# One run of kv products and adjacent attention halves in a linear-attention kernel

## What is computed

```python
def feature_map(x, orf):
    proj = x @ orf.T / d_k ** 0.25
    norm = jnp.sum(x * x, axis=-1, keepdims=True) / (2.0 * math.sqrt(d_k))
    return (jnp.exp(proj - norm) + EPS) / math.sqrt(m)
q = feature_map(split(x @ Wq.T + bq), orf)
k = feature_map(split(x @ Wk.T + bk), orf)
v = split(x @ Wv.T + bv)
kv = jnp.einsum('nlm,nld->nmd', k, v)
ksum = jnp.sum(k, axis=1)
buf = jnp.concatenate([kv, ksum[..., None]], axis=-1)
out = jnp.einsum('nlm,nmd->nld', q, buf)
out = out[..., :-1] / out[..., -1:]
...
return out @ Wo.T + bo
```

## Time and profile before

| | us |
|---|---|
| median of 3 runs | 1294.16 |
| lowest, highest | 1293.69, 1294.86 |
| the profiled execution | 1294.25 |
| its span | 1292.4 |
| PE, DVE, ACT, POOL busy | 1271.0, 940.0, 701.2, 327.8 |

### The profile page before, as it was taken

The page is one execution under the profiler, slowest core; times in us unless marked ns, Lnnn a source line. Parts: engine busy times, 40 slices in busy tenths (PEclk is TensorE's granted clock), DMA queues, the critical chain, the costliest instruction groups (busy, mean ns, idle before and its releaser), DMA issues.

```text
span 1292.4 us, 24909 instructions
## 1 busy us (share of the span) xinstructions
PE 1271.0 (98%) x8626; PEld 958.5 (74%) x8626; DVE 940.0 (73%) x1775; ACT 701.2 (54%) x1403; POOL 327.8 (25%) x617
## 2 busy tenths in 40 slices
PE   9999999999999999999999999999999999999986
PEld 8767787777877678776787768876788767887655
DVE  6599765886668875788657886587875788657876
ACT  5557535564356743657336663367534665446534
POOL 0102332024310333103421034211253022420043
PEclk9999999999999999999999999999999999999999
DMA  6658314773146821567215762257612686036611
GB/s 232 147 137 222 95 47 110 180 184 88 58 115 164 201 67 51 135 163 189 62 58 130 181 168 67 64 130 204 158 46 72 144 208 151 27 83 146 162 54 65
DMA packets 82749, 160.33 MB, mean 124 GB/s; under 512 B 17856, under 2 KB 36416, under 8 KB 82112
## 3 DMA queue, kind: packets, MB, share of 16 engines
q1 hardware_dynamic: 68880, 139.78, 43.7%
q10 hardware_dynamic: 9648, 16.85, 3.5%
q0 software_dynamic: 4096, 2.11, 0.7%
HBM read 39.13 MB, written 16.78 MB: 43 GB/s over the span
## 4 chain that ended last, share of the span: by engine, by line
PE 87%; ACT 5%; DVE 4%; issue 3%; POOL 0%; ACTq 0%; POOLq 0%; DVEq 0%
PE ps L946 26%; PE ps L909 18%; PE ps L959 8%; PE ps L1009 8%; PE ps L932 5%; PE ps L934 5%; PE ps L933 5%; PE ps L977 4%; PE ps L964 4%; ACT features L663 2%; PE ps L1035 2%; ACT x_hi L631 1%; PE ps L904 1%; DVE squares_turned L819 0%; ACT unit_hi L644 0%
## 5 line engine op out<-in xcount | busy, mean ns | idle before, releaser
L663 ACT ACTIVATE features<-ps 128x512 f32<-128x512 f32 x512 | 279.0, 604 | 249.3 <-PE ps L959 192.2
L565 POOL DMA_DIRECT2D stacks<-norm_rows x128 | 69.7, 548 | 530.0 <-DVE norm_rows L834 283.9
L959 PEld LDWEIGHTS ps<-orf_stack,stacks 98*128 98x128 f32 x1024 | 131.3, 191 | 29.8 <-issue 21.7
L909 PE MATMUL ps<-Wo_hi,stacks 128*128 128x512 f32 x448 | 150.4, 402 | 0.0
L636 ACT ACTIVATE values_then_attention<-ps 128x512 f32<-128x512 f32 x64 | 38.3, 599 | 198.0 <-PE ps L934 195.0
L775 DVE TENSOR_TENSOR den<-den,features 128x512 f32<-128x512 f32 x186 | 128.1, 689 | 12.8
L959 PE MATMUL ps<-orf_stack,stacks 98*128 98x128 f32 x1024 | 132.0, 272 | 0.0
L1009 PE MATMUL ps<-features,kv_ksum 128*32 128x512 f32 x1024 | 123.1, 598 | 3.4 <-ACT features L663 2.2
L811 DVE SCALAR_TENSOR_TENSOR unit_lo<-ps,cols,unit_hi 128x512 fp32r<-128x512 f32 x128 | 94.2, 736 | 36.3 <-ACT squares L646 36.3
L545 POOL TENSOR_SCALAR stats<-stats 128x1 f32<-128x1 f32 x128 | 36.3, 283 | 331.7 <-DVE stats L762 331.5
L946 PE MATMUL ps<-x_hi,Wk_hi 128*128 128x512 f32 x256 | 109.7, 429 | 1.5 <-DVE x_lo L804 1.4
(11 more groups left out here) (132 smaller groups left out, 2534.0 us busy)
## 6 DMA issues: line engine op xcount, KB each, us to landing
stacks<-unit_hi SPq DMA_DIRECT2D x512, 128.0 KB, 2.4
stacks<-unit_lo SPq DMA_DIRECT2D x256, 128.0 KB, 3.0
out<-rows ACTq DMA_DIRECT2D x56, 256.0 KB, 2.0
rows<-in_x_t SPq DMA_DIRECT2D x49, 256.0 KB, 3.4
rows<-in_x SPq DMA_DIRECT2D x32, 256.0 KB, 4.0
features<-in_x SPq DMA_DIRECT2D x32, 256.0 KB, 4.0
values_then_attention<-in_x_t SPq DMA_DIRECT2D x8, 256.0 KB, 7.4
stacks<-norm_rows POOLq DMA_DIRECT2D x128, 16.0 KB, 3.0
```

The lines of the kernel that those rows point to most:

```text
L565: pool.dma_start(slot[row:row + 1, :].rearrange("o (t c) -> o t c", c=DH), NN[:, u % 2, part, :].bitcast(F32)).then_inc(n_lifted[u % 2].se ...
L663: nc.scalar.activation(FE[:, n % 8, :, 0:M], ps[:, :].rearrange("p (a m) -> p a m", a=HG), ACT.Exp, scale=C_EXP).then_inc(a_exp.sem, 1)
L909: last = mm(out, a, b, start=(n == 0), stop=(n == len(terms) - 1))
L959: last = mm(ps[:, M * h:M * (h + 1)], slot[0:QK, L * h + P * r:L * h + P * (r + 1)], ORF[0:QK, h, :], start=True, stop=True)
```

## The change

All eight kv products of a group now stand in the query unit, after the first two feature stages; only the last group of the last batch keeps four and four. In query units 1, 3 and 5 the two attention products stand side by side, after the projections, and both scalings (R) after the norms. In unit 7 they stay apart. The second half's denominators go to a bank of the feature ring; the feature stage that gets this bank next waits for VectorE's transposing of them, and the second half no longer waits for bank 7.

```diff
--- before.py
+++ after.py
@@ -60,6 +60,11 @@
     return b + 1 == B and g + 1 == NG
 
 
+def split_at(b, g):
+
+    return 4 if sums_on_pe(b, g) else 0
+
+
 def is_key(u):
     return u % 2 == 0
 
@@ -91,7 +96,7 @@
     lift = [("LIFT", *two), ("NL", *two)] if two else []
     if is_key(u):
         st = [[("ST", b - 1, t)] if u == 0 and b else [] for t in (TT - 2, TT - 1)]
-        half = [("G", b, g, r) for r in range(4)]
+        half = [("G", b, g, r) for r in range(split_at(b, g))]
         early = [("AG", b, 0, 0), ("AG", b, 1, 0)] if b + 1 == B and u + 2 == NU else []
         if u == 0:
             seq = f(0, 1) + p[1] + s0 + l0 + f(2, 3) + q0 + st[0] + p[2] + f(4, 5) + half + s1 + l1 + f(6, 7) + q1 + norm + lift
@@ -105,21 +110,22 @@
         if u == 2 and 0 < b < B - 1:
             seq += [("LX", b + 1, t) for t in range(5)]
         return seq
-    kv = [("G", b, g, r) for r in range(4, 8)]
+    kv = [("G", b, g, r) for r in range(split_at(b, g), 8)]
     if u < NU - 1:
         seq = p[0] + f(0, 1)
         if u == 1 and b == 0:
             seq += [("WS", 0)]
         if b + 1 == B and u == NU - 3:
-            seq += p[1] + s0 + l0 + kv + f(2, 3) + p[2] + f(4, 5) + s1 + q0 + [("KVT", b, g)] + f(6, 7) + l1 + [("GG", b, g, 0)] + q1 + norm + lift
-            seq += [("GG", b, g, 1), ("R", b, g, 0)] + [("LR", b, t) for t in range(4)]
+            seq += p[1] + s0 + l0 + kv + f(2, 3) + p[2] + f(4, 5) + s1 + q0 + [("KVT", b, g)] + f(6, 7) + l1 + q1 + norm + lift
+            seq += [("GG", b, g, 0), ("GG", b, g, 1), ("R", b, g, 0)] + [("LR", b, t) for t in range(4)]
         elif u < NU - 3:
-            seq += kv + f(2, 3) + p[1] + [("KVT", b, g)] + s0 + l0 + f(4, 5) + p[2] + f(6, 7) + s1 + q0 + [("GG", b, g, 0)]
-            seq += l1 + p[3] + [("R", b, g, 0), ("GG", b, g, 1)] + q1 + norm + lift
+            seq += kv + f(2, 3) + p[1] + [("KVT", b, g)] + s0 + l0 + f(4, 5) + p[2] + f(6, 7) + s1 + q0
+            seq += l1 + p[3] + [("GG", b, g, 0), ("GG", b, g, 1)] + q1 + norm + lift + [("R", b, g, 0)]
         else:
             seq += xt(0) + kv + f(2, 3) + p[1] + [("KVT", b, g)] + s0 + l0 + xt(1, 2) + f(4, 5) + xt(3)
-            seq += [("LX", b + 1, t) for t in range(5, TT)] + p[2] + [("GG", b, g, 0), ("R", b, g, 0)] + q0
-            seq += s1 + xt(4) + f(6, 7) + xt(5) + l1 + p[3] + xt(6, 7) + [("GG", b, g, 1)] + q1 + norm + lift
+            seq += [("LX", b + 1, t) for t in range(5, TT)] + p[2] + q0
+            seq += s1 + xt(4) + f(6, 7) + xt(5) + l1 + p[3] + xt(6, 7) + [("GG", b, g, 0), ("GG", b, g, 1)] + q1 + norm + lift
+            seq += [("R", b, g, 0)]
             seq += [("LR", b, t) for t in range(4)]
         seq += [("R", b, g, 1)] if b + 1 < B or u < NU - 3 else []
         if u == 1 and b == 0:
@@ -209,6 +215,8 @@
         return (0, 1) if stage[2] < 2 else (0, 1, 2, 3, 4)
     if stage[0] in ("YT", "FF") and stage[1] + 1 == B:
         return (0, 1, 2, 3, 4)
+    if stage[0] == "GG":
+        return (2, 3, 4) if stage[3] else None
     return RING.get(stage[0])
 
 
@@ -413,6 +421,8 @@
                 return v_ln[1], v_ln[1].nth(b, 3 * k + 1)
             if kind == "F":
                 return a_exp, a_exp.nth(b, 8 * k + stage[3] + 1)
+            if kind == "GG":
+                return v_dt, v_dt.nth(b, 2 * k + 2)
             return v_ylo, v_ylo.nth(b, k + 1)
 
         BANKING = bank_uses(SCHEDULE)
@@ -842,7 +852,8 @@
                     n, den = 2 * (2 * g + h), by_token[h]
                     dve.wait_ge(t_gg.sem, t_gg.nth(b, 2 * g + h + 1))
                     dve.wait_ge(v_a.sem, v_a.nth(b, 2 * g + h - 1))
-                    nc.vector.transpose(turned[:, :, 0:DH], DN[:, :].rearrange("p (a c) -> p a c", c=DH)).then_inc(v_dt.sem, 1)
+                    dens = ps if h else DN
+                    nc.vector.transpose(turned[:, :, 0:DH], dens[:, :].rearrange("p (a c) -> p a c", c=DH)).then_inc(v_dt.sem, 1)
                     dve.wait_ge(v_dt.sem, v_dt.nth(b, 2 * g + h + 1))
                     dve.wait_ge(a_c.sem, a_c.nth(b, 2 * g + 2))
                     nc.vector.reduce_sum(den, turned[:, :, DH - 1:DH + 1], axis=mybir.AxisListType.X).then_inc(v_dr.sem, 1)
@@ -998,13 +1009,13 @@
                     if half == 0:
 
                         pe.wait_ge(v_kvc.sem, v_kvc.nth(b, g + 1))
+                        pe.wait_ge(v_dt.sem, v_dt.nth(b, 2 * g))
                     else:
                         pe.wait_ge(v_a.sem, v_a.nth(b, 2 * g))
                         if b == 0 and g == 0:
                             pe.wait_ge(s_scale, 1)
-                    pe.wait_ge(v_dt.sem, v_dt.nth(b, 2 * g + half))
                     pe.wait_ge(a_exp.sem, a_exp.nth(b, 16 * g + 8 + 4 * half + 4))
-                    for bank, c in ((DN, P), (ND[half], 0)):
+                    for bank, c in ((ps if half else DN, P), (ND[half], 0)):
                         for h in range(HG):
                             last = mm(bank[DH * h:DH * (h + 1), :], KVS[:, g % 2, c + DH * h:c + DH * (h + 1)],
                                       FE[:, HG * half + h, :, 0:M], start=True, stop=True, tile_position=(0, DH * h))
```

## The result

| | before | changed |
|---|---|---|
| median us | 1294.51 (4 runs) | 1337.05 (4 runs, 1336.99 to 1337.24) |
| span of the profiled execution | 1292.4 | 1335.2 |
| mean granted clock | 0.999 | 0.989 |

The ratio is 1.033, 95% interval 1.0318 to 1.0344. The direction was right; the size was not: +42.5 us between these medians, where I forecast +32.2 on the profiled execution's 1294.25. The time is 1 us outside the stated range.

The account below looks back on a forecast made before the run. TensorE, busy 98% of the span, was taken to bound the kernel. Terms 14.9 + 17.7 - 1.9 + 2.4 - 0.9 = +32.2 us on the profiled 1294.25 gave 1326.5 us, range 1312 to 1336.

Parts of the forecast that it names:

- units 1 to 2 and 3 to 4: Eight batches, 16 times: kv gain 0.24, attention gain 0.30, new unit_lo wait 1.47; +0.93 each, +14.9 us in all.
- units 5 to 6, seven batches: Unit 5 loses 1.30, unit 6 waits 1.47, less kv gain 0.24: 2.53 each, seven times, +17.7 us.
- ternary slices: First batch, ends of units 1 and 3: VectorE's 1.22 us weight slice adds to the wait; +2.4 us in all.
- last batch's wait for the turned denominators: Last batch: the second attention half no longer waits for the first half's turned denominators; 0.9 us gained.
- The one more scaling on VectorE: Key units: one more scaling, 1.47 us, stands ahead of unit_lo, so TensorE waits 1.47 us there, 23 times.
- the hole in unit 5: Seven batches: the moved attention product no longer covers ScalarE's x split; TensorE waits about 1.6 us for x_lo, net +1.30.
- rival (e): TensorE's clock halves behind the new waits: 2.8 us more in each of 23 units, 1390 us; chance 2%.
- the ring bank that holds the denominators: Third feature stage: bank turned before TensorE wants it, costed at nothing; without cover up to 0.85 us in 32 groups.
- (a): Key units: the mergers gain with no new wait, the first half's scaling being covered; 1279 us, chance 7%.
- (b): Key unit's wait is real, but unit 5 has no hole because ScalarE's split starts earlier; 1315.3 us, chance 8%.
- (c): Only unit 5's hole is real, VectorE catches up elsewhere; 1290.2 us, chance 4%.
- (d): TensorE's switches shrink less than the rows suggest: 54 mergers give 5.4 instead of 14.3 us; 1335.4 us, chance 10%.

Follow-up runs that it names:

- kv alone: The kernel before with the eight kv products in one run, attention halves and their scaling left where they were: 1294.53 us, ratio 1.0001.
- the run with the later scaling: The changed kernel with the second half's scaling moved behind the next key unit's unit_lo: 1319.8 us, ratio 1.0200.
- kv alone with the last batch's order: Kernel before with kv in one run, VectorE's unit_lo earlier, squares later, ternary slices moved, last batch's unit 5 kv run before the second projection: 1285.47 us, ratio 0.994.
- unit 5 as before: The changed kernel with unit 5's first attention product and its scaling back ahead of the later projections: 1315.84 us, ratio 1.0173.
- shifted: The changed kernel with twelve more transposes in the first batch's unit 1, putting everything behind them 1.3 us later: 1336.45 us, ratio 1.0338.
- the halves alone: The changed kernel with the kv products back in two halves, attention halves still joined: 1319.55 us, ratio 1.0199.

## Why the prediction was right and wrong

The steps of the table give the whole, 42.8 us of span:

| term | forecast | measured |
|---|---|---|
| units 1 to 2 and 3 to 4 | 16 x 0.93 = 14.9 | 15 x 0.82 + 0.45 = 12.8 |
| units 5 to 6, seven batches | 17.7 | 17.2 |
| unit 0 | -1.9 | -1.8 |
| ternary slices | 2.4 | 2.4 |
| last batch's wait for the turned denominators | -0.9 | 0 |
| half-clock stretches | 0 | 12.3 |

(The 0.45 is the last batch's second step, 27.32 - 25.28, without its half-clock stretch: that run of twelve projections took 4.45 us instead of 2.86. The 12.3 are four times in the first batch 1.40, 1.56 and 2.98 for two, in three others 1.59, 1.63 and 1.60, and 1.59 in the last. How the first batch's first two steps divide into slices and half-clock stretches is worked out from the 0.82 of the other batches, not measured apart.)

**Right.** The one more scaling on VectorE, the place and count of the wait, its size (1.41 against 1.47), the hole in unit 5 (2.50 against 2.53 for the step), and that both mergers do gain on TensorE what the switches cost: 0.30 per group for kv (forecast 0.24; kv alone, 23.50 to 23.20), and for the attention halves 0.28 (forecast 0.30), which is 23.50 - 0.30 + 1.41 less the 24.33 measured. Taking the scaling away removed the wait (the run with the later scaling), restoring unit 5 removed the hole, and both together removed the loss.

**Wrong: rival (e) was priced at 2%, and it came on top of the forecast.** The step that failed was: "The granted clock stays at the 2.4 GHz level through all slices, with waits of up to 2.1 us in the waits view near the end, so 1.5 us should not do it." By it the clock went into the sum at nothing; it measured 12.3 us. I compared the longest single wait. In unit 5 there are two waits close together (0.67 and 1.32 us with 1.8 us between the two starts), then 1.4 in unit 6, and in the first batch waits of 2.4; of the four old waits near the end only one was of 2.1 us. Absence in one profile with few holes was taken for proof. That one absence was luck, as other runs show: the same wait stands in every kernel here, and in six of the twelve others (among them kv alone with the last batch's order) a half-clock stretch begins within 0.6 us of its end. The wait before and 3.2 us behind it, then the same in kv alone with the last batch's order:

```profile
1277.59 0.41 PE L1035 MATMUL ps<-ident,values_then_attention 128*128 128x128 f32 x2 [2.07 <-ACT values_then_attention L611]
1278.00:1281.20 3.20, 2.05 (x10) 1.37 (x8) 1.81 (x4) 1.99 (x3) 1.04 (x3) 1.00 0.04 13
```

```profile
1268.39 0.41 PE L1040 MATMUL ps<-ident,values_then_attention 128*128 128x128 f32 x2 [2.06 <-ACT values_then_attention L616]
1268.80:1272.00 3.20, 3.20 (x10) 2.44 (x8) 0.75 (x2) 1.98 (x3) 1.03 (x3) 0.50 0.04 13
```

The rival was also priced all or nothing, at 23 units of 2.8 us; it came eight times at 1.5 us. Without it the sum is 30.5 and the time would have been within 2 us of the forecast. The Trainium skill, "TensorE: Matmul & The Clock Gate", Part 1, which rival (e) cites, says an idle TensorE is granted half its clock. The traces agree in part: the grant was 0.50 at the holes, but at 609.80 it was 0.50 while TensorE was busy through the whole 3.20 us.

**Wrong: the last batch.** The 0.9 us I credited didn't show: from the end of its third group's kv run to the end of the span are 79.19 us, against 79.22 before. The wait for the turned denominators went, but the next two releases stood right behind it, 0.55 and 0.31 us:

```profile
1262.09 1.92 PE L1020 MATMUL ps<-features,kv_ksum 128*32 128x512 f32 x16 [0.55 <-ACT features L673]
...
1265.36 1.90 PE L970 MATMUL ps<-orf_stack,stacks 98*128 98x128 f32 x15 [0.31 <-DVE dens_turned L856]
```

The second is the ring bank that holds the denominators. It was costed at nothing, and that held everywhere but here.

**Right, with a slip.** The slack that unit_lo had before, "about 1.3 us", is 1.15 by the prediction's own times (TensorE at T + 8.97, the bank free at 708.52 + 0.74 + 0.15, T + 7.82). The sum doesn't use it. But it was taken from unit 2 alone and believed of every key unit, which the run with kv alone paid for.

Rivals (a), (b) and (c) are out: there was no free cover, the hole was there seven times, and the key unit's waits 23 times. So is (d): each merger gained what the rows gave.

What stays open: which waits bring a fall. Single waits of 1.4 us did so in no middle batch (unit 5 as before), though the stretches at 138.7 and 1248.0 in the changed kernel stand behind one. Unit 5's hole did in three of six middle batches in the changed kernel, in three when shifted (the fifth in both), in five of six with the halves alone and in all with the scaling later. And some stretches in last batches stand behind waits of under 0.6 us (1244.3 with unit 5 as before, 1264.1 when shifted). Nor are these falls the changed kernel's alone: executions of the kernel before took from 1292.8 us at a granted clock of 0.999 to 1296.4 at 0.996.

## What to carry to other kernels

When work moves out of a stretch on the busiest engine, it arrives earlier at the next buffer; compute that arrival and the releaser's chain together, in every unit that has the pattern, since the slack differed from 1.2 to 0.5 us between units that run the same code. A move of two parts of one stage next to each other also puts the consumer's work for both in a row: look for the release that stands behind them in the consumer's order, and move that up; this and unit 5's old order turned 1337 us into 1291; kv alone with the same moves and the last batch's order took 1285. And price an idle TensorE by more than its idle time: here unit 5's hole of 2 us cost 1.5 us more in 20 of the 28 batches that had it in four kernels, and a single wait of 1.4 us in 2 of 21 in the changed kernel. One profile without a fall doesn't show that a wait of that length is safe.

## What the runs showed of the hardware

Each half-clock stretch ahead of the kernel's end lasted 3.4 us and cost 1.4 to 1.6 us. In the changed kernel six of the eight began 0.1 to 1.3 us after the wait, with TensorE already working again (at 609.8, with products running since 609.31), and two 0.2 to 0.3 us before the wait's end (80.7, 121.6). The distance between two 128x512 projections was 0.43 us in it and 0.23 outside. With twelve more transposes in the first batch, 1.3 us, others of the equal holes were followed by one, and the first batch had one instead of four; but the executions of that kernel also differed among themselves (1335.5 us at a granted clock of 0.992, 1339.9 at 0.989). Changing between products on the whole array and on a quarter of its columns cost 0.08 to 0.09 us going in, 0.11 coming out, and 0.05 to 0.11 at the first product behind; sixty-four kv records in one run took 1.78 us by the changed kernel's timeline, where two runs of thirty-two took 1.02 and 0.91.
